# A 1024-wide spin-attention and FFN layer on eight cores: layernorm of the first tiles over three engines, a third buffer for transposed blocks, and FFN weights loaded after the last transposes of P

## What is computed

```python
xn = layernorm(x)                                  # eps 1e-5
s  = xn @ W_spin.T + b_spin
g  = mean(s, over tokens) @ W_global               # one row
e  = s @ W_J.T
P  = softmax((e @ s.T) / 32)
a  = tanh(beta * (s + g + P @ s))
x1 = x + layernorm(a)
y  = layernorm(x1)
h  = silu(y @ wg.T / 127) * (y @ wu.T / 127)       # hidden 3072, int32 weights
x2 = x1 + layernorm(h @ wd.T / 127)
```

## Time and profile before

| | |
|---|---|
| time, median of 3 runs | 1162.86 us (1162.45 to 1163.61) |
| profiled execution | 1164.29 us; span of its slowest core (core 0) 1162.7 us |
| spans of the other cores | 1156.0 to 1159.3 us |
| PE busy | 1118.1 us (96%) |
| DVE busy | 448.0 us (39%) |
| ACT busy | 260.4 us (22%) |
| POOL busy | 97.5 us (8%) |
| mean granted TensorE clock, core 0 | 0.991 |

### The profile page before, as it was taken

How to read it: one execution, slowest core, us unless ns; L and a number is a source line. 1 busy time by engine, 2 the same in 40 slices (tenths; PEclk the granted TensorE clock), 3 DMA queues, 4 the chain that set the end, 5 groups by cost and what they waited for, 6 DMA issues and landing times.

```text
span 1162.7 us, 15068 instructions; the slowest of 8 cores (1156.0 to 1162.7 us)
## 1 busy us (share of the span) xinstructions
PE 1118.1 (96%) x5097; PEld 509.2 (44%) x5200; DVE 448.0 (39%) x1141; ACT 260.4 (22%) x458; POOL 97.5 (8%) x130
## 2 busy tenths in 40 slices
PE   3999999899999999999999899999999999999997
PEld 2444444344444444444444344444444444444443
DVE  5364710235555555555555531211212121233333
ACT  4434443211112222211112111111111111111111
POOL 4000001001111111111112100010000000000000
PEclk9999999999999999999999899999999999999999
DMA  9894769923343343444434434444542220323321
GB/s 204 194 217 110 181 103 163 204 37 82 82 100 83 82 85 88 91 87 94 97 88 81 91 64 73 74 74 81 81 73 37 37 37 1 130 88 109 109 91 54
DMA packets 172219, 112.15 MB, mean 96 GB/s; under 512 B 146416, under 2 KB 148464, under 8 KB 172144
## 3 DMA queue, kind: packets, MB, share of 16 engines
q1 hardware_dynamic: 151824, 65.03, 24.6%
q0 software_dynamic: 19168, 41.95, 18.9%
q10 hardware_dynamic: 1152, 4.19, 1.1%
HBM read 83.89 MB, written 16.78 MB: 87 GB/s over the span
## 4 chain that ended last, share of the span: by engine, by line
PE 88%; SPq 6%; DMA 2%; issue 1%; ACT 1%; DVE 1%; ACTq 0%; DVEq 0%
PE ps L472 18%; PE ps L453 17%; PE ps L531 14%; PE ps L509 14%; PE ps L502 14%; PE ps L437 8%; SPq L260 5%; PE ps L424 2%; DMA pT<-S_sb 2%; SPq L224 1%; DMA xnT<-xn 0%; ACTq L540 0%; PE ps L388 0%; ACT xn L558 0%; DVE st L685 0%
## 5 line engine op out<-in xcount | busy, mean ns | idle before, releaser
L472 PE MATMUL ps<-s_tok,pT 128*128 128x512 bf16 x1004 | 225.3, 382 | 5.8 <-DMA pT<-S_sb 4.8
L453 PE MATMUL ps<-s_FM,eT 128*128 128x512 bf16 x1004 | 224.5, 381 | 6.5 <-DVE S_sb L738 5.4
L509 PE MATMUL ps<-xn2T,wgu 128*128 128x512 bf16 x753 | 180.1, 379 | 0.8
L502 PE MATMUL ps<-xn2T,wgu 128*128 128x512 bf16 x752 | 179.9, 379 | 0.8
L531 PE MATMUL ps<-wdT_sb,h_act 128*128 128x512 bf16 x753 | 165.1, 379 | 0.8
L813 DVE SCALAR_TENSOR_TENSOR h_act<-silu_b,ps 128x512 bf16<-128x512 f32 x96 | 65.9, 688 | 251.7 <-PE ps L509 251.2
L472 PEld LDWEIGHTS ps<-s_tok,pT 128*128 128x128 bf16 x1024 | 100.9, 99 | 127.9 <-issue 9.1
L453 PEld LDWEIGHTS ps<-s_FM,eT 128*128 128x128 bf16 x1024 | 100.5, 98 | 127.9 <-issue 8.3
L593 ACT ACTIVATE S_sb<-S_sb,nmx 128x1024 bf16<-128x1024 f32 x64 | 72.7, 1136 | 224.2 <-DVE nmx L747 224.2
L606 ACT ACTIVATE silu_b<-ps 128x512 f32<-128x512 f32 x96 | 57.3, 597 | 269.2 <-PE ps L502 259.2
L509 PEld LDWEIGHTS ps<-xn2T,wgu 128*128 128x128 bf16 x768 | 75.2, 98 | 90.6
(11 more groups left out here) (80 smaller groups left out, 515.8 us busy)
## 6 DMA issues: line engine op xcount, KB each, us to landing
xs<-x SPq DMA_DIRECT2D x24, 512.0 KB, 5.9
xr<-x POOLq DMA_DIRECT2D x16, 512.0 KB, 5.4
x_sc<-xr POOLq DMA_DIRECT2D x16, 512.0 KB, 3.0
x1b<-x_sc SPq DMA_DIRECT2D x16, 512.0 KB, 3.7
out<-ob SPq DMA_DIRECT2D x15, 512.0 KB, 3.7
wgu<-wg POOLq DMA_DIRECT2D x24, 256.0 KB, 4.1
wgu<-wu POOLq DMA_DIRECT2D x24, 256.0 KB, 4.8
wdT_sb<-wdT POOLq DMA_DIRECT2D x6, 1024.0 KB, 10.2
```

Source lines behind the costliest of these rows:

```text
L453: mm = pe.matmul(bank(2 * slot + half), eT[:, j, t * P:(t + 1) * P], s_FM[:, j, m0:m0 + 512], start=(j == 0), stop=(j == KC - 1))
L472: mm = pe.matmul(bank(pv_bank(t) + nb), pT[:, m, :], s_tok[:, m, nb * 512:(nb + 1) * 512], start=(m == 0), stop=(m == NT - 1))
L502: mm = pe.matmul(bank(n % 4), wgu[:, hb % 3, 0, j, :], xn2T[:, j, tb * 512:(tb + 1) * 512], start=(j == 0), stop=(j == KC - 1))
L509: mm = pe.matmul(bank(4 + n % 4), wgu[:, hb % 3, 1, j, :], xn2T[:, j, tb * 512:(tb + 1) * 512], start=(j == 0), stop=(j == KC - 1))
```

## The change

The tiles 0 to 7 are scaled by the engine that the string `SCALED_BY` names ("d" VectorE, "a" ScalarE, "p" GpSimd): VectorE 0, 4 and 7, ScalarE 2, 5 and 6, GpSimd 1 and 3. The last two stand in GpSimd's program ahead of the weight loads, which also wait for the seventh x tile instead of the sixth. VectorE takes the statistics of tile k before it takes the reciprocal of tile k-1, and it computes the bias `nb0` for every tile. `xnT` has three buffers, the third in memory that had been free in this phase; the transposes of block b wait for the matmuls of block b-3. On GpSimd the six loads of the first FFN weights stand behind the addition of iteration t = 16 and wait also for the last transpose of P. The rest only follows: the counts in waits on `v_xn`, `a_xn` and the new `l_xn`.

```diff
+SCALED_BY = "dpapdaad"
...
-        xnT = at("xnT", [P, 2, KC, 512], BF16, 144 * KB)
+        xnT = [at("xnT_0", [P, KC, 512], BF16, 144 * KB),
+               at("xnT_1", [P, KC, 512], BF16, 152 * KB),
+               at("xnT_2", [P, KC, 512], BF16, 192 * KB)]
...
+        def scaled(k):
+
+            e = SCALED_BY[k]
+            return ({"d": v_xn, "a": a_xn, "p": l_xn}[e],
+                    SCALED_BY[:k + 1].count(e))
+
+        ND0 = SCALED_BY.count("d")
...
-                sp.wait_ge(v_xn, NPT // 2 + k - NPT + 1)
-                sp.wait_ge(p_grp, DONE[("s", b - 2)])
+                sp.wait_ge(v_xn, ND0 + k - NPT + 1)
+                if b >= 3:
+                    sp.wait_ge(p_grp, DONE[("s", b - 3)])
                 sp.dma_start_transpose(
-                    out=xnT[:, b % 2, :, (k % 4) * P:(k % 4 + 1) * P],
+                    out=xnT[b % 3][:, :, (k % 4) * P:(k % 4 + 1) * P],
...
                 if g == 0:
-                    sp.wait_ge(v_xn, NPT // 2 + NT - NPT)
-                    sp.wait_ge(a_xn, NPT // 2)
+                    sp.wait_ge(v_xn, ND0 + NT - NPT)
+                    sp.wait_ge(a_xn, SCALED_BY.count("a"))
+                    sp.wait_ge(l_xn, SCALED_BY.count("p"))
...
-            gp.wait_ge(d_x[5], 16)
+            for k in range(NPT):
+                if SCALED_BY[k] == "p":
+                    gp.wait_ge(v_rb0, k + 1)
+                    gp.tensor_scalar(out=xn[:, k, :], in0=xs[:, k, :],
+                                     scalar1=mv0[:, 2 * k:2 * k + 1],
+                                     scalar2=ri0[:, k:k + 1],
+                                     op0=ALU.subtract, op1=ALU.mult
+                                     ).then_inc(l_xn, 1)
+            gp.wait_ge(d_x[6], 16)
...
             for t in range(1, NQ + 2):
-                if t == NQ:
-                    gp.wait_ge(p_qk, 4 * NQ)
-                    for hb in range(3):
-                        gp.dma_start(out=wgu[:, hb, 0], in_=wg_d[hb]
-                                     ).then_inc(d_gu[hb], 16)
-                        gp.dma_start(out=wgu[:, hb, 1], in_=wu_d[hb]
-                                     ).then_inc(d_gu[hb], 16)
...
                     gp.tensor_tensor(out=sg[:], in0=s_tok[:, t - 1, :],
                                      in1=g_bc[:], op=ALU.add
                                      ).then_inc(l_sg, 1)
+                if t == NQ:
+                    gp.wait_ge(p_qk, 4 * NQ)
+                    gp.wait_ge(d_pT[3], 16 * NQ)
+                    for hb in range(3):
+                        gp.dma_start(out=wgu[:, hb, 0], in_=wg_d[hb]
+                                     ).then_inc(d_gu[hb], 16)
+                        gp.dma_start(out=wgu[:, hb, 1], in_=wu_d[hb]
+                                     ).then_inc(d_gu[hb], 16)
...
-                if k % 2 == 1:
-                    s.wait_ge(v_rb0, k // 2 + 1)
+                if SCALED_BY[k] == "a":
+                    s.wait_ge(v_rb0, k + 1)
...
-            def apply0(k):
+            def stats0(k):
+                o = 12 * (k % 4)
+                v.wait_ge(d_x[k], 16)
+                v.bn_stats(out=st6[:, o:o + 6], in_=xs[:, k, 0:512])
+                mark(v.bn_stats(out=st6[:, o + 6:o + 12],
+                                in_=xs[:, k, 512:1024]))
+                settle()
+                v.bn_aggr(out=mv0[:, 2 * k:2 * k + 2],
+                          in_=st6[:, o:o + 12]).then_inc(v_var0, 1)
+
+            def scale0(k):
                 v.wait_ge(a_sd0, k + 1)
                 mark(v.reciprocal(out=ri0[:, k:k + 1], in_=sd0[:, k:k + 1]))
                 settle()
-                if k % 2 == 0:
+                v.scalar_tensor_tensor(out=nb0[:, k:k + 1],
+                                       in0=mv0[:, 2 * k:2 * k + 1],
+                                       scalar=-1.0, in1=ri0[:, k:k + 1],
+                                       op0=ALU.mult, op1=ALU.mult
+                                       ).then_inc(v_rb0, 1)
+                if SCALED_BY[k] == "d":
                     v.tensor_scalar(out=xn[:, k, :], in0=xs[:, k, :],
                                     scalar1=mv0[:, 2 * k:2 * k + 1],
                                     scalar2=ri0[:, k:k + 1],
                                     op0=ALU.subtract, op1=ALU.mult
                                     ).then_inc(v_xn, 1)
...
-                apply0(k)
+
+            stats0(0)
+            for k in range(1, NPT):
+                stats0(k)
+                scale0(k - 1)
+            scale0(NPT - 1)
```

More of the change, by code:

```diff
@@ L114, in build_program @@
         a_xn = sem("a_xn")
+        l_xn = sem("l_xn")
         a_xnT = sem("a_xnT")
@@ L230, in x_load @@
                 if old >= NPT:
-                    sp.wait_ge(v_xn, NPT // 2 + old - NPT + 1)
-                elif old % 2 == 0:
-                    sp.wait_ge(v_xn, old // 2 + 1)
+                    sp.wait_ge(v_xn, ND0 + old - NPT + 1)
                 else:
-                    sp.wait_ge(a_xn, old // 2 + 1)
+                    sp.wait_ge(*scaled(old))
                 sp.dma_start(out=xs[:, k % XSLOTS, :], in_=x_t[k]
@@ L382, in tile_transposes @@
             def tile_transposes(k):
-                if k % 2 == 0:
-                    pe.wait_ge(v_xn, k // 2 + 1)
-                else:
-                    pe.wait_ge(a_xn, k // 2 + 1)
+                pe.wait_ge(*scaled(k))
                 for j in range(KC):
@@ L400, in moving @@
                     if kind == "s":
-                        return xnT[:, b % 2, i, :]
+                        return xnT[b % 3][:, i, :]
                     return s_FM[:, i, b * 512:(b + 1) * 512]
@@ L547, in xnT_copy @@
                 s.wait_ge(p_tr, k + 1)
-                s.copy(out=xnT[:, k // 4, :, (k % 4) * P:(k % 4 + 1) * P],
+                s.copy(out=xnT[k // 4][:, :, (k % 4) * P:(k % 4 + 1) * P],
                        in_=tbank(k).rearrange("p (j f) -> p j f", f=P)
@@ L663, in vec_prog @@
             mark(v.memset(eps_col[:], EPS))
-            def apply0(k):
-                v.wait_ge(a_sd0, k + 1)
-                mark(v.reciprocal(out=ri0[:, k:k + 1], in_=sd0[:, k:k + 1]))
-                settle()
-                if k % 2 == 0:
-                    v.tensor_scalar(out=xn[:, k, :], in0=xs[:, k, :],
-                                    scalar1=mv0[:, 2 * k:2 * k + 1],
-                                    scalar2=ri0[:, k:k + 1],
-                                    op0=ALU.subtract, op1=ALU.mult
-                                    ).then_inc(v_xn, 1)
-                else:
-                    v.scalar_tensor_tensor(out=nb0[:, k:k + 1],
-                                           in0=mv0[:, 2 * k:2 * k + 1],
-                                           scalar=-1.0, in1=ri0[:, k:k + 1],
-                                           op0=ALU.mult, op1=ALU.mult
-                                           ).then_inc(v_rb0, 1)
-            for k in range(NPT):
+            def stats0(k):
                 o = 12 * (k % 4)
@@ L690, in vec_prog @@
                           in_=st6[:, o:o + 12]).then_inc(v_var0, 1)
-                apply0(k)
+            def scale0(k):
+                v.wait_ge(a_sd0, k + 1)
+                mark(v.reciprocal(out=ri0[:, k:k + 1], in_=sd0[:, k:k + 1]))
+                settle()
[5 more added lines that the diff above has]
+                if SCALED_BY[k] == "d":
+                    v.tensor_scalar(out=xn[:, k, :], in0=xs[:, k, :],
+                                    scalar1=mv0[:, 2 * k:2 * k + 1],
+                                    scalar2=ri0[:, k:k + 1],
+                                    op0=ALU.subtract, op1=ALU.mult
+                                    ).then_inc(v_xn, 1)
+            stats0(0)
[3 more added lines that the diff above has]
+            scale0(NPT - 1)
             v.wait_ge(v_var0, NPT)
@@ L720, in vec_prog @@
                                     ).then_inc(v_xn, 1)
-                v.wait_ge(v_xn, NPT // 2 + 4 * b + 4 - NPT)
+                v.wait_ge(v_xn, ND0 + 4 * b + 4 - NPT)
             v.wait_ge(a_ev, DONE[("s", 7)])
```

## The result

The changed kernel takes 1150.78 us (median of 4 runs, 1150.56 to 1151.27) against 1162.97 (1162.45 to 1163.61): a ratio of 0.9896 with a 95% interval of 0.9878 to 0.9913. It is 12.2 us faster, where 16 were forecast. The profiled execution took 1150.8 us; its slowest core is now core 4 with a span of 1149.3 us, and the eight spans lie between 1147.6 and 1149.3.

What follows compares the result with a forecast made beforehand. TensorE, busy 1118.1 of 1162.7 us, was taken as the bound, leaving only idle and low-clock time: 1164.29 - 7.3 - 7.5 - 1.2 = 1148.3, less 1.4 for the median gives 1146.9 us. Range 1143.8 to 1154.5.

Steps and rivals of the forecast that it cites:

- two large terms: TensorE's waits near 225 and 633 us with the low clock after them: gains of 7.3 and 7.5 us.
- part 3: Start: reordered statistics, tiles 1 and 3 scaled on GpSimd; tile 7's transposes at 32.1 against 32.48, gain 1.2 us.
- first rival: Start: GpSimd scales slowly, P = 4.3, so 4.5 us lost instead of 1.2 won, 1152.6 us; chance 0.14.
- Part 1: Attention near 225 us: a third xnT buffer lets pT(0) go out with its exp; stall and low clock go, 7.3 us.
- Part 2: End of attention near 633 us: six wgu loads moved behind the last pT transpose; stall and low clock go, gain 7.5 us.
- low-clock term: TensorE's slow matmuls after the two stalls: 5.36 - 3.45 near 225 us, 9.92 - 6.91 = 3.0 near 633 us.
- likeliest case: Whole kernel: all three places gain as forecast, 1146.9 us, own span 1144 to 1150; chance 0.70.
- Slower than before: GpSimd's queue at the start: P of about 10.5 us uses up the gain; at 11 us about 1166; chance 0.02.
- full stall at 225: TensorE idle 5.43 us behind L738 until 230.73, as pT(0) waits in SyncE's queue behind s_tok transposes; to go whole.

Runs made afterwards that it cites:

- dpadadad: The changed kernel with only tile 1 scaled on GpSimd, ScalarE scaling tile 4 and VectorE tile 5: 1148.59 us, ratio 0.9868.
- dpdadada: Against the kernel with VectorE and ScalarE scaling in turn, tile 1 alone moved to GpSimd: 1147.32 us, ratio 0.9864.
- dadadada: The changed kernel with VectorE and ScalarE scaling the tiles in turn, none on GpSimd, weight loads behind the sixth x tile: 1145.16 us, ratio 0.9851.
- dddddddd: The changed kernel with all eight tiles scaled by VectorE, weight loads behind the sixth x tile: 1144.21 us, ratio 0.983.
- dddddddd, roots first: The all-VectorE kernel with ScalarE doing the roots of tiles 5 to 7 before it copies tiles 4 to 7: 1143.89 us, ratio 0.9836.
- old start: The changed kernel with the start as in the kernel before: VectorE and ScalarE alternating, no pipelining, GpSimd only loading: 1148.99 us, ratio 0.9881.

## Why the prediction was right, and where not

The direction and the two large terms were right. The time lies 3.9 us above the forecast: about 3 are part 3, forecast as a gain of 1.2 us and measured as a loss of some 2, and the rest is in parts 1 and 2, which gave 14.0 of 14.8. It also lies above the forecast's own span of 1144 to 1150; the range holds it because the first rival was taken in.

**Part 1** was forecast at 7.3 us; undoing it costs 7.6. The steps: s_tok starts at 148 and not near 140, since the x loads came 8 us later (block 2's transposes begin at 66.5, before at 58.1), not 3. It still ended in time, and pT(0) went out with its exp, as forecast.

**Part 2** was forecast at 7.5; undoing it costs 8 (7.6 by the spans). In both parts the forecast set a merged row (5.36, 9.92) against distances (3.45, 6.91), which makes each low-clock term 0.17 us too large. The last two transposes land in 3.0 and 4.6 us. The tight place that was named, xn2T of tile 15 at the seventh unit, is there: on core 4 that unit starts 1.91 us after the product before it, where the distance is 1.73 elsewhere; 0.18 us were lost, 0.3 forecast.

By the Trainium skill (page "DMA: Bandwidth & Descriptors", section "Queues, rings and completion order") a DMA engine goes round-robin between the queues with work, packet by packet. The forecast took this to mean "about twice 3.4 us" for a transpose, and so no stall. That step was wrong, and the runs don't refute the rule itself: the step took all packets to last equally long. The DMA view of the kernel before, core 0, 630 to 652 us, with the six loads and the last two pT transposes under way (queue: packets, MB, share of the time of 16 engines):

```profile
q0 software_dynamic: 1152, 2.62, 59.5%
q1 hardware_dynamic: 4429, 1.09, 31.8%
```

q0 carries GpSimd's transfers (its 2.62 MB are the six loads of 256 KB and two transfers of 512 KB), q1 those of SyncE. By these shares a packet of q0 takes 0.18 us and one of q1 0.025 us. A transpose has a little over 1000 packets (146416 under 512 B for 136 transposes in the whole profile), some 65 for each engine. If each of them waits for one packet of the loads, the transpose takes 65 x 0.21, some 13 us (an estimate); 13.7 and 14.9 were measured. So the wait is of the size that packet-by-packet turns give, but no run separates this from another way of holding a transpose. What the runs do show is the dependence: six loads early 14.25 us of queue, two loads 7.90, none 4.68.

**Part 3** is the term that failed. Forecast: a gain of 1.2 us with P = 1.5. The step is the bound of P from above, "2.14 us, GpSimd's two-input f32 addition of the same shape". P, the time of one GpSimd scaling, is 3.78 us. The estimate from the Trainium skill (page "GPSIMD Engine Reference", section "Performance versus the Vector engine"), 0.9 us plus dispatch, was further off still: this instruction takes 3.78 us and even with one operation 2.84; only the copy, 1.04 us, is near its figure. The rival "GpSimd scales slowly" had P = 4.3, a loss of 4.5 us and 1152.6; with P = 3.78 its own rule of 2 us for each us gives 1 us less of loss, about 1151.6, and 1150.8 was measured. So the likeliest case didn't happen in this part and the first rival did, with its mechanism and nearly its price. Its slope was measured by doubling P, 7.4 us of span for 7.6 us of added work.

The forecast let the first matmul hang on the wspT loads. It did, on all eight cores, but with tile 3's copy only 1.0 us ahead on the mean, so that issuing the loads 6.7 us earlier changed nothing. In the rival "Slower than before" a sum is off: by its own rule the 18.3 us are used up at P = 10.85, not at 10.5.

**The sum.** The kernels with parts 1 and 2 share one number: from the start of the last sixteen matmuls of the first group to the end of the span. With a full clock in the sixteen it is 1112.4 to 1113.0 us:

| kernel | sixteen start at, slowest core | span | difference |
|---|---|---|---|
| changed kernel | 36.66 | 1149.3 | 1112.6 |
| each scaling twice | 44.16 | 1156.7 | 1112.5 |
| two wgu loads early | 36.58 | 1149.2 | 1112.6 |
| weight loads between the scalings | 36.06 | 1149.1 | 1113.0 |
| dpadadad | 34.56 | 1147.0 | 1112.4 |
| dpdadada | 32.71 | 1145.2 | 1112.5 |
| dadadada | 31.90 | 1144.4 | 1112.5 |
| dddddddd | 29.77 | 1142.2 | 1112.4 |
| dddddddd, roots first | 29.64 | 1142.1 | 1112.5 |

The slowest core of the old start lies 1114.0 behind its 33.19, the 1.5 more being the low clock of its sixteen. The forecast without part 3, 1164.29 less 7.3 and 7.5, is 1149.5, and the profiled execution with the old start took 1148.8. So with parts 1 and 2 in place each us of the start is a us of the time. In the kernel before, core 0 was slowest by 3.4 us: it had the longest wait for the first tile, the full stall at 225 and the low clock in its sixteen together; now the eight cores lie within 1.7 us.

The best kernels of this study are the all-VectorE ones: 1144.21 and 1143.89 us, ratios 0.983 (0.9815 to 0.9846) and 0.9836 (0.9822 to 0.9851), 19 us below the kernel before and some 7 below the changed one.

## What to carry to other kernels

Look not only at who uses the late transfer but at what stands ahead of it in its queue, plain loads on another engine's queue included: moving six loads behind two transposes gave 8 us and a buffer more gave 7.6, each without touching the work of the bound engine. Before giving work to an engine that stands at the head of a chain and in front of its own DMA issues, measure that very instruction there; the price of a neighbouring one is no bound, and a fast chain can be shorter with fewer engines. When a stage is bound from a point on, record the distance from that point to the end: it turns every experiment on the stage before into one subtraction.

## What the runs showed of the hardware

- On GpSimd, for a tile of 128x1024 in f32: subtract and multiply by per-row scalars 3.78 us, by constants 3.63, one operation 2.84, two-input multiplication 2.35, copy to bf16 1.04. VectorE does the first in 0.81.
- DMA transposes issued behind plain casting loads of GpSimd's queue are held: 4.68 us of queue for two without loads, 7.90 behind two loads, 14.25 behind six. By the shares of the DMA view a packet of the loads' queue took 0.18 us, one of the transposes' queue 0.025.
- The clock after a short wait differs from core to core: behind the same wait of 2.28 to 2.29 us the same sixteen matmuls took 3.62 us on three cores and 5.01 to 5.30 on five, in one execution. Behind waits of at most 1.1 us they took 3.62 on all eight cores of twelve kernels.
